# Attention pooling on one core: the second layer one pair later in TensorE's order, and the softmax steps of a group at later places

## What is computed

```python
B, L, D, H = 2048, 200, 128, 64
qe = broadcast_to(q[:, None, :], k.shape)
feat = concatenate([qe, k, qe - k, qe * k], axis=-1)
h = feat @ W1 + b1                        # H = 64 columns
h = where(h >= 0, h, alpha[0] * h)
a = (h @ W2 + b2)[..., 0]
a = where(mask == 0, NEG, a)
w = softmax(a, axis=-1)
y = einsum('bl,bld->bd', w, k)            # r_k is 2048 x 200 x 128 f32, 210 MB
```

## Time and profile before

| | |
|---|---|
| median of 3 runs | 1007.28 us (1003.37 to 1023.59) |
| the profiled execution | 1010.41 us |
| its span on the core | 1008.3 us |
| granted TensorE clock, mean | 0.979 of full speed |
| PE / DVE / POOL / ACT busy | 85% / 76% / 65% / 53% of the span |
| the core's DMA queue for data | 65.5% of 16 engines' span |
| read from HBM | 214.57 MB, 217 GB/s over the span |
| exponentials of the 32 groups | first at 57.4 us, last at 988.8 us: 30.05 us from one to the next |

### The profile page before, as it was taken

One profiled execution on the slowest core, in us unless ns is written; L12 is line 12 of the kernel. 1 busy time (PEld: TensorE's weight loads), 2 busy tenths in 40 slices (PEclk: granted clock), 3 DMA queues, 4 the chain that ended last, 5 costly groups with the idle time before them and its releaser, 6 DMA issues.

```text
span 1008.3 us, 55360 instructions
## 1 busy us (share of the span) xinstructions
PE 852.4 (85%) x25216; PEld 560.0 (56%) x25216; DVE 769.5 (76%) x1143; ACT 533.8 (53%) x1281; POOL 656.2 (65%) x401
## 2 busy tenths in 40 slices
PE   2779889888889888889888898898898889888896
PEld 1445556555556555556555565565565556555564
DVE  5988867878878778778677778788778778777871
ACT  0556545555545555555554555565556555555552
POOL 3667656767667667667666676676676666667761
PEclk9999999999999999999899999999999999999999
DMA  8847667667677767677665777666777666777620
GB/s 256 338 145 229 217 231 234 230 221 246 198 240 244 231 218 238 201 237 242 232 202 180 239 235 236 213 216 231 239 242 242 231 213 209 242 262 235 225 94 11
DMA packets 67017, 222.45 MB, mean 221 GB/s; under 512 B 25312, under 2 KB 33504, under 8 KB 66784
## 3 DMA queue, kind: packets, MB, share of 16 engines
q1 hardware_dynamic: 66784, 218.92, 65.5%
HBM read 214.57 MB, written 4.33 MB: 217 GB/s over the span
## 4 chain that ended last, share of the span: by engine, by line
PE 38%; DMA 18%; DVE 16%; issue 13%; ACT 7%; SPq 7%; POOL 0%; DVEq 0%; ACTq 0%; POOLq 0%
PE hP L435 22%; DMA keys<-in_r_k 11%; DVE act L350 9%; PE poolP L478 8%; PE scoreP L466 7%; DMA probs_scratch<-expd 6%; ACT act L289 5%; DVE keysT L342 5%; SPq L160 3%; SPq L211 3%; ACT expd L315 2%; DVE neg_max L363 1%; PE poolP L487 1%; DVE logits L357 1%; DMA keys<-in_r_q 1%
## 5 line engine op out<-in xcount | busy, mean ns | idle before, releaser
L289 ACT ACTIVATE act<-hP,biast,al 128x200 f32<-128x200 f32 x1024 | 460.3, 514 | 352.7 <-PE hP L435 349.1
L342 DVE STREAM_TRANSPOSE keysT<-keys 128x768 f32<-128x768 f32 (+1 forms) x512 | 510.0, 997 | 60.8 <-DMA keys<-in_r_k 60.6
L435 PE MATMUL hP<-keysT,weff 32*64 32x200 f32 x16384 | 482.8, 346 | 38.3 <-issue 30.3
L232 POOL TENSOR_TENSOR weff<-qX,wp 128x1024 f32<-128x1024 f32 x128 | 243.9, 1906 | 315.6 <-PE hP L435 299.7
L435 PEld LDWEIGHTS hP<-keysT,weff 32*64 32x64 f32 x16384 | 312.7, 134 | 201.5 <-issue 129.3
L350 DVE TENSOR_TENSOR act<-hP,act 128x400 f32<-128x400 f32 x512 | 283.8, 554 | 144.8 <-ACT act L289 140.7
L236 POOL TENSOR_TENSOR weff<-weff,wk 128x1024 f32<-128x1024 f32 x128 | 303.3, 2369 | 10.0
L478 PE MATMUL poolP<-keys,pool_w 128*16 128x128 f32 x6400 | 242.7, 276 | 18.4 <-issue 16.9
L478 PEld LDWEIGHTS poolP<-keys,pool_w 128*16 128x16 f32 x6400 | 172.7, 97 | 91.4 <-issue 86.7
L466 PE MATMUL scoreP<-act,w2win 128*16 128x200 f32 x2048 | 150.0, 342 | 73.9 <-DVE act L350 69.8
L271 POOL TENSOR_TENSOR pool_w<-probs_k,own_b 128x400 f32<-128x400 f32 x128 | 111.2, 869 | 15.7 <-PE poolP L478 7.9
(11 more groups left out here) (35 smaller groups left out, 29.7 us busy)
## 6 DMA issues: line engine op xcount, KB each, us to landing
keys<-in_r_k SPq DMA_DIRECT2D x128, 832.0 KB, 5.7
keys<-in_r_k SPq DMA_DIRECT2D x128, 768.0 KB, 5.2
probs_scratch<-expd SPq DMA_DIRECT2D x32, 100.0 KB, 4.0
masks<-in_r_mask SPq DMA_DIRECT2D x128, 12.5 KB
probs_k<-probs_scratch SPq DMA_DIRECT2D x128, 12.5 KB
out_rows<-pooled SPq DMA_DIRECT2D x128, 8.0 KB
keys<-in_r_q SPq DMA_DIRECT2D x4, 256.0 KB, 5.1
act<-in_L_rec_W SPq DMA_DIRECT2D x4, 128.0 KB, 6.4
```

What stands on the lines that cost most here:

```text
L232: g_.tensor_tensor(weff[:, n % 2, :, :, :], qX[:, n, :, :].unsqueeze(3).broadcast_to([P, BQ, CD, H]), wp[:].unsqueeze(1).broadcast_to([P, ...
L289: a_.activation(act[:, k, a, :], hP[:, 2 * (p % HSETS) + a % 2, 0:L], ACT.Identity, bias=biast[:, n, k, a:a + 1], scale=al[:]).then_inc(t_ ...
L342: v_.transpose(keysT[:, n % TBUF, j0 * D:j1 * D], keys[:, n % SLOTS, j0 * D:j1 * D]).then_inc(keysT_done, 1)
L435: mm = t_.matmul(hP[H * r:H * r + H, 2 * (p % HSETS) + a % 2, 0:L], weff[QP * a:QP * a + QP, n % 2, w, c, :], kT[QP * a:QP * a + QP, :, c, ...
```

## The change

On TensorE, S(n, 0) goes from the end of step n to behind f0 of step n+1, and S(n-1, 1) from before f2 to behind f2. The order of a full step becomes f0, S(n-1, 0), f1, P head, f2, S(n-1, 1), f3, P tail. On VectorE the mask and the maximum go from behind activate(4n) to behind activate(4n+1), and the reciprocal of the row sums goes to the next step. On ScalarE the exponential and the new fill go from before pair 4n+1 to the end of the step, behind pair 4n+2. On SyncE the round trip of the probabilities goes to step 4g+5: out to DRAM ahead of key part 0, the wait and the four DMAs back between part 0 and part 1; and the mask's DMAs go one step later, to 4g+6. Nothing is added or taken away.

```diff
 # SyncE
                     sp.wait_ge(part_done, n + AHEAD - SLOTS + 1)
+                g = n // GT - 1
+                if n % GT == 1 and 0 <= g < GROUPS:
+                    sp.wait_ge(exp_done, g + 1)
+                    ge(sp, poolw_done, (g - 1) * GT)
+                    sp.dma_start(probs_dram[g % 2], expd[:, g % 2, :]).then_inc(probs_out, 16)
                 paced_part(0)
-                g = n // GT - 1
-                if n % GT == 1 and 0 <= g < GROUPS - 2:
+                if n % GT == 1 and 0 <= g < GROUPS:
+                    sp.wait_ge(probs_out, (g + 1) * 16)
+                    for t in range(GT):
+                        sp.dma_start(probs_k[:, g % 2, t, :], probs_tiles[g % 2, t]
+                                     ).then_inc(probs_in[GT * (g % 2) + t], 16)
+                if n % GT == 2 and 0 <= g < GROUPS - 2:
                     sp.wait_ge(scores_read, g + 1)
                     load_mask(g + 2)
                 for x in range(1, LOADS // 2 + 1):
                     paced_part(x)
-                if n % GT == 0 and 0 <= g < GROUPS:
-                    sp.wait_ge(exp_done, g + 1)
-                    ge(sp, poolw_done, (g - 1) * GT)
-                    sp.dma_start(probs_dram[g % 2], expd[:, g % 2, :]).then_inc(probs_out, 16)
-                    sp.wait_ge(probs_out, (g + 1) * 16)
-                    for t in range(GT):
-                        sp.dma_start(probs_k[:, g % 2, t, :], probs_tiles[g % 2, t]
-                                     ).then_inc(probs_in[GT * (g % 2) + t], 16)
 # ScalarE: the block "if n % GT == 0" with L312 to L319 (exponential, fill) stands
 # behind scale_pair(PAIRS * n + 1) and scale_pair(PAIRS * n + 2); L320 to L327 (pooled) stay before them
 # VectorE
                 activate(PAIRS * n)
-                if group:
-                    mask_scores(g)
-                transpose_piece(n + 2, 0)
-                activate(PAIRS * n + 1)
-                if group:
+                if n % GT == 1 and 0 <= g < GROUPS:
                     dve.wait_ge(exp_done, g + 1)
                     ge(dve, pooled_moved, g - 1)
                     v_.reciprocal(inv_sum[:, g % 2:g % 2 + 1], exp_sum[:, g % 2:g % 2 + 1]).then_inc(inv_done, 1)
+                transpose_piece(n + 2, 0)
+                activate(PAIRS * n + 1)
+                if n % GT == 0 and 0 <= g < GROUPS:
+                    mask_scores(g)
                 transpose_piece(n + 2, 1)
 # TensorE
+                if n <= TILES:
+                    first_layer(PAIRS * n)
+                if 0 <= n - 1 < TILES:
+                    second_layer(n - 1, 0)
                 if n < TILES:
-                    first_layer(PAIRS * n)
                     first_layer(PAIRS * n + 1)
-                if n == TILES:
-                    first_layer(PAIRS * n)
                 if late and m <= TILES:
                     add_parts(m // GT - 1)
                 if 0 <= m < TILES and not late:
                     pool_keys(m, 0, HEAD_J)
+                if n < TILES:
+                    first_layer(PAIRS * n + 2)
                 if 0 <= n - 1 < TILES:
                     second_layer(n - 1, 1)
                 if n < TILES:
-                    first_layer(PAIRS * n + 2)
                     first_layer(PAIRS * n + 3)
                 if 0 <= m < TILES:
                     pool_keys(m, 0 if late else HEAD_J, J)
-                if n < TILES:
-                    second_layer(n, 0)
```

More of the change, by code:

```diff
@@ L309, in _ @@
                     fill(0)
+                if m % GT == GT - 1 and 0 <= m < TILES:
+                    g = m // GT
+                    act_e.wait_ge(pooled_done, g + 1)
+                    act_e.wait_ge(inv_done, g + 1)
+                    ge(act_e, out_done[g % 2], g // 2 * 16 * QUADS)
+                    a_.activation(pooled[:, g % 2, :], poolP[:, D:2 * D], ACT.Copy,
+                                  scale=inv_sum[:, g % 2:g % 2 + 1]).then_inc(pooled_moved, 1)
+                scale_pair(PAIRS * n + 1)
+                scale_pair(PAIRS * n + 2)
                 g = n // GT - 1
@@ L319, in _ @@
                         fill(g + 1)
[L320 to L329, removed]
         @block.vector
@@ L408, in _ @@
                 g = n // GT - 1
-                group = n % GT == 0 and 0 <= g < GROUPS
                 transpose_piece(n + 1, 2)
```

## The result

The changed kernel takes 956.34 us (median of 4 runs, 950.4 to 966.5) against 1008.4 for the kernel before, measured beside it (4 runs). Some executions of a kernel fall into a slower state, and ratios are taken over the others, here without the one of 966.5. The ratio is 0.9497, with a 95% interval of 0.9428 to 0.9566: 5.0% faster. The forecast was 920 us, with 878 to 975 as its range. The gain is real, but little more than half of the forecast's 8.7%.

The account below looks back on a forecast made before the run. A latency loop inside steps and a group loop through late keys and the probabilities' round trip bound the kernel. 13.17 + 12.17 + 1.89 gave period 27.23; 31 periods plus ends, 921.0 span, gave 920 us, range 878 to 975.

Parts of the forecast that it names:

- The latency loop: Within an ordinary step, PE, ScalarE and VectorE wait in turn around each activated pair; it binds at 6.05 us a step.
- a step's work is 5.68: TensorE's new order: calls, scores, pooling head and tail add to 5.68 us a step, against 6.05 now.
- Mask, maximum, exponential: Same instructions moved later: exponential 6.00 us after f0, ScalarE waits for nothing, PE's 1.28 us wait behind it goes.
- The stall: PE's wait behind the exponential, 1.28 us in the group shown, claimed to go once the exponential moves.
- the forecast's loop: Once per group: late keys, steps, exponential, probabilities' round trip in SP's queue, then the next late keys; period 30.05 us now.
- SP's queue: Write, four DMAs back, then part 1, masks off the path: keys at 18.17 us, f0 of step 4g+7 at 19.66.
- the sum: Per group: 13.17 us from keys to exponential, 12.17 from exponential to keys, 1.89 unexplained; period 27.23.
- The third rival: The probabilities' write to DRAM returns sooner, leg 3.2 us or less; period 26.1, about 885 us; chance 0.15.
- the key loop: The once-per-group path from late keys through exponential and round trip to the next late keys, taken as binding at 27.23 us.
- the 1.89 of unexplained time: Remainder of the present group period beyond the counted 28.16 us, containing PE's gaps without a cause; kept unchanged at 1.89.
- The fourth rival: PE reads instructions faster, so bubbles return as causeless gaps and late keys; period 30.6, no change; chance 0.09.
- The first rival: Keys limit every step: at a landing of 6.3 us, period 28.7, about 966 us; chance 0.18.

Follow-up runs that it names:

- e1: The kernel before with only TensorE's new order; mask, exponential and SyncE's queue at their old places: 1014.69 us, ratio 1.0037 to the kernel before.
- q3: The changed kernel with TensorE's old order and most of the key traffic left out (stale keys): 876.46 us, ratio 0.8714 to the kernel before.
- e6: The kernel before with only mask, maximum, exponential, fill and reciprocal at their new places: 1018.03 us, ratio 1.0105 to the kernel before.
- q1: The changed kernel with most key traffic left out, 3 of 12 or 13 columns per load from the tenth tile: 870.87 us, ratio 0.8653.
- e4: The changed kernel with half the pooling head put into the middle of call f1, two more switches: 973.15 us, ratio 0.9614.
- q4: The changed kernel with half the pooling head inside call f1 and most key traffic left out: 916.74 us, ratio 0.9114 to the kernel before.
- q2: The changed kernel with pooling directly behind scores (four switches a step), VectorE's pieces in twos, most key traffic left out: 893.44 us, ratio 0.8883.
- e5: The kernel before with only the four mask DMAs moved one step later, behind key part 0: 980.75 us, ratio 0.9746 to the kernel before.

## Why the prediction was right in sign and too large

**The latency loop.** The loop was read rightly, and so was its removal: PE's waits for the activated pair before the score records are nearly gone. The step "a step's work is 5.68" failed: it is 6.14. It took a call of `first_layer` at 0.79 from two in a row, and the tail by its count. Rows 3 to 5 hold the same kinds of records with other neighbours, and cannot show what four more switches cost: 6.14 - 5.68 = 0.46 per step. The gain of 0.37 a step became a loss of 0.09, and e1 and q3 show that nothing is left of it.

**Mask, maximum, exponential.** The stall went as forecast. In the step shown the exponential starts 6.21 after f0 (6.00 forecast), and ScalarE does not wait before it:

```profile
478.93 0.46 ACT L326 ACTIVATE expd<-logits,neg_max 128x200 f32<-128x200 f32 x1
```

Alone the move gains nothing and costs 1% (e6); of the 40 us that the forecast's loop would charge for it, 11 came.

**SP's queue.** This is the part that pays, and in the group shown its timetable held. Counted from that f0, the keys came at 490.38, +17.66 (forecast 18.17), and f0 of step 4g+7 at 492.20, +19.48 (forecast 19.66):

```profile
490.38 0.98 DVE L343 STREAM_TRANSPOSE keysT<-keys 128x768 f32<-128x768 f32 x1 [1.30 <-DMA keys<-in_r_k]
...
492.20 0.92 PE L435 MATMUL hP<-keysT,weff 32*64 32x200 f32 x28
493.65 0.56 PE L435 MATMUL hP<-keysT,weff 32*64 32x200 f32 x4 [0.54 <-issue]
...
499.15 0.58 PE L435 MATMUL hP<-keysT,weff 32*64 32x200 f32 x12 [0.69 <-issue]
```

Over all groups that wait for keys they come 11.1 us behind the exponential (mean), where the sum had 12.17: the write is back sooner, so that part 1 is issued at 5.9 instead of 6.75. Masks and part 0 left the path as forecast. The rows of SP's queue in that group, with part 0 at 479.91 ahead of the probabilities and the masks behind part 0 of the next step:

```profile
479.54 0.33 SPq L202 DMA_DIRECT2D probs_scratch<-expd  x1
479.91 0.44 SPq L152 DMA_DIRECT2D keys<-in_r_k  x1
...
483.29 2.27 SPq L207 DMA_DIRECT2D probs_k<-probs_scratch  x4
485.61 0.95 SPq L152 DMA_DIRECT2D keys<-in_r_k  x2
486.60 2.73 SPq L160 DMA_DIRECT2D masks<-in_r_mask  x4
```

**The third rival** was half right. The write returned sooner: over the 32 groups it took 2.7 us on average from its issue to the four DMAs back (3.75 in the group above), inside the 3.2 that the rival gave, against 3.85. The Trainium skill's rule on a semaphore's increment (DMA: Bandwidth & Descriptors, Queues, rings and completion order) made that forecast, and the trace agrees: in none of 27 groups, before or after, does the write land ahead of the part 1 that was issued ahead of it. It landed 0.35 us behind that part before (median) and lands 1.6 us behind it now, so the part held it then and mostly does not now. It bought nothing by itself, since the key loop no longer decides: VectorE waits for keys in half of the groups.

**The sum.** After 492.20 the next f0 came at 500.64, 8.44 later, where the sum had 5.68: 0.46 is the switches, the rest the two gaps at 493.65 and 499.15. The forecast's period of 27.23 was that of the key loop alone, with the 1.89 of unexplained time kept. TensorE's own sum was 4 x 5.68 = 22.7 and seemed far away. In truth it is 25.5 (q1), and late instruction packets, with some 5 us from the lower clock, bring it to 28.06: that is the bound, and it is 0.83 x 31 = 26 us above the forecast. Of the other 10 us, 2 are in the two ends (59.2 and 19.7 against 57.4 and 19.5), and the rest is that the profiled execution, 950.4, is 6 us below this kernel's median, where the forecast scaled by 0.997. The fourth rival (0.09) named the right thing, PE's reading of its instructions, but not its course: the recorded gaps did not double, they stayed at 1.5 us per group (47.7 against 49.2 in all). The time is in the range because the bound that the forecast left out, PE's own work with its gaps, stood only 0.83 us per group above the loop that it counted; that is luck. The first rival came out nearest in time (966) for another reason; keys were not late in every step.

## What to carry to other kernels

- When one queued wait holds the load that everybody needs, look at what stands in that queue between wait and load. Moving four small DMAs behind it brought 2.5%, and no instruction of any computing engine was touched. But a load that is issued 2.8 us earlier, close behind another, may land only 1.0 us earlier.
- A reordering on TensorE is costed by segments with their neighbours, not by records: put pieces with the same rows of the array side by side, and add up the busy engine's whole new sum beside the loop that is being shortened.
- In a program written out in full, PE's instruction stream is a consumer of DMA. If gaps stand at equal numbers of instructions and end behind a packet of the instruction queue, less data traffic is what helps; here a PE slowed by two more switches had 40 of them instead of 67.
- Read the granted clock beside the waits: a pause of PE that is followed by the lower clock costs more than its own length.

## What the runs showed of the hardware that I had not expected

- A change between matmuls whose weights fill 32 partitions and matmuls whose weights fill 128 costs PE about 0.1 to 0.25 us, with no wait recorded: 6.14 against 5.68 for four more per step, and 0.50 for two between short segments (e4, and 45.9 us in all in q4). A change between score and pooling records, both of 128 rows, costs 0.11 less (0.35 against 0.46, q2).
- PE's instructions come late under key traffic, as inferred from counts and packet times: 47.7 us of recorded gaps, which make some 66 us of time between the first and the last exponential; 4.6 us of recorded gaps are left when the traffic falls to a third (q1). The packets move as fast as in q1 (0.96 us), but start later.
- Slowing PE by 45 us cost only about 12 us (2 to 22) under full traffic (e4 beside q4).
- A key load that is issued 2.8 us earlier, close behind another one, took 6.9 instead of 5.1 us to land (e5).
